# Half of the value products ahead of the transposes, and the scaled features made by ScalarE

## What is computed

```python
h = (node_features @ W_proj.T).reshape(B, N, H, dh)
scores = s_left[:, :, None, :] + s_right[:, None, :, :] + adjacency[..., None] * we
scores = leaky_relu(scores, 0.2) + (NEG * (adjacency <= 1e-05))[..., None]
agg = einsum('bijh,bjhd->bihd', softmax(scores, axis=2), h).reshape(B, N, D)
out = leaky_relu(node_features + agg + bias, 0.5)      # then x + out, and a layer norm
```

## Time and profile before

| | |
|---|---|
| median of 3 runs | 1983.24 us (1981.75 to 1984.76) |
| the profiled execution | 1981.11 us |
| its span | 1979.2 us |
| POOL busy | 1866.3 us (94%), 663 instructions |
| DVE busy | 1821.9 us (92%) |
| PE busy | 1795.4 us (91%) |
| ACT busy | 1646.4 us (83%), 3895 instructions |

### The profile page before, as it was taken

How to read it: one execution, slowest core, us unless ns; L and a number is a source line. 1 busy time by engine, 2 the same in 40 slices (tenths; PEclk the granted TensorE clock), 3 DMA queues, 4 the chain that set the end, 5 groups by cost and what they waited for, 6 DMA issues and landing times.

```text
span 1979.2 us, 34310 instructions
## 1 busy us (share of the span) xinstructions
PE 1795.4 (91%) x11080; PEld 875.2 (44%) x11080; DVE 1821.9 (92%) x3413; ACT 1646.4 (83%) x3895; POOL 1866.3 (94%) x663
## 2 busy tenths in 40 slices
PE   7799999999999999899999999999999999878885
PEld 6544444444444444445444444444444444333332
DVE  3699999999999999999999999999999999999997
ACT  6788887899888898888988889888887898676674
POOL 3599999999999999999999999999999999999995
PEclk9899999999999999999999999999999999999999
DMA  3232315233243243333233331333315233333310
GB/s 100 73 115 91 102 50 157 83 114 106 66 138 99 81 120 100 94 113 99 79 120 100 86 119 58 121 121 91 102 54 156 81 113 91 102 96 96 102 54 11
DMA packets 138090, 190.63 MB, mean 96 GB/s; under 512 B 22328, under 2 KB 56504, under 8 KB 137912
## 3 DMA queue, kind: packets, MB, share of 16 engines
q1 hardware_dynamic: 137912, 188.44, 31.8%
HBM read 179.77 MB, written 8.65 MB: 95 GB/s over the span
## 4 chain that ended last, share of the span: by engine, by line
POOL 28%; ACT 20%; PE 19%; issue 17%; DVE 15%; SPq 0%; DMA 0%; ACTq 0%; DVEq 0%; POOLq 0%
POOL X L501 26%; PE psum L1217 15%; DVE X L1102 11%; ACT E L773 4%; PE psum L1396 3%; ACT psum L776 3%; ACT pen L734 3%; ACT squares L642 2%; DVE X L1091 2%; POOL haug L484 1%; ACT blk L590 1%; ACT blk L563 1%; ACT x1s L670 1%; ACT o_sb L670 0%; ACT act_T L563 0%
## 5 line engine op out<-in xcount | busy, mean ns | idle before, releaser
L501 POOL TENSOR_TENSOR X<-RHO,E 128x1536 f32<-128x1536 f32 (+1 forms) x512 | 1779.3, 3506 | 41.8 <-ACT E L773 35.3
L1102 DVE SCALAR_TENSOR_TENSOR X<-psum,s_j,X 128x512 f32<-128x512 f32 x2048 | 1397.4, 741 | 78.8 <-POOL X L501 68.0
L1217 PE MATMUL psum<-X,haug 128*33 128x512 f32 x4096 | 978.6, 598 | 8.2 <-ACT accU L752 4.6
L1396 PEld LDWEIGHTS psum<-ident,adj_sb 128*128 128x128 f32 x2048 | 285.9, 140 | 561.8 <-DVE X L1102 429.1
L1396 PE MATMUL psum<-ident,adj_sb 128*128 128x128 f32 x2048 | 430.6, 291 | 101.3 <-DVE X L1102 97.7
L773 ACT ACTIVATE E<-psum,we_s 128x512 f32<-128x512 f32 x512 | 395.5, 772 | 139.0 <-PE psum L1217 137.1
L1217 PEld LDWEIGHTS psum<-X,haug 128*33 128x33 f32 x4096 | 195.0, 110 | 431.7 <-issue 390.6
L776 ACT ACTIVATE psum<-psum,we_s 128x512 f32<-128x512 f32 x512 | 380.7, 744 | 0.0
L1217 PE MATMUL psum<-sgn_ident,pen 128*128 128x128 bf16 x2048 | 374.7, 219 | 0.0
L734 ACT ACTIVATE pen<-adj_sb,pen_bias 128x512 bf16<-128x512 f32 x512 | 366.8, 717 | 1.0 <-PE psum L1217 0.2
L1091 DVE TENSOR_TENSOR X<-psum,E 128x512 f32<-128x512 f32 x496 | 334.0, 673 | 3.6 <-ACT RHO L563 2.2
(11 more groups left out here) (231 smaller groups left out, 1547.5 us busy)
## 6 DMA issues: line engine op xcount, KB each, us to landing
adj_sb<-in_adj_dram SPq DMA_DIRECT2D x128, 1024.0 KB, 5.2
RHO<-rho_scratch SPq DMA_DIRECT2D x31, 1024.0 KB, 9.7
out_dram<-o_sb SPq DMA_DIRECT2D x32, 256.0 KB, 2.3
xg<-in_x_dram SPq DMA_DIRECT2D x28, 256.0 KB, 5.3
blk<-in_adj_dram SPq DMA_DIRECT2D x56, 64.0 KB, 5.1
X<-in_x_dram SPq DMA_DIRECT2D x2, 256.0 KB, 3.0
W_sb<-in_L_gnn_W_dram SPq DMA_DIRECT2D x4, 64.0 KB, 2.1
X<-in_adj_dram SPq DMA_DIRECT2D x4, 64.0 KB, 2.8
```

Source lines behind the costliest of these rows:

```text
L501: Q.tensor_tensor(X[m % NX][:, 0:heads, :], RHO[:, g % 2, 0:heads, :], bc(E[m % NE][:], 1, [P, heads, GROUP]), ALU.mult).then_inc(B_pool, 1)
L1102: ins = V.scalar_tensor_tensor(slot[:, h, :], TA[m % NT], s[:, k, h:h + 1], slot[:, h, :], ALU.mult, ALU.max)
L1217: return T.matmul(o, l, r, start=start, stop=stop)
L1396: T.matmul(o, adj_sb[c][:, t, at:at + P], ident[:], is_transpose=True, start=True, stop=False)
```

## The change

Four things:

- `values` is cut in two. `values(m, 0)`, heads 0 and 1, stands in front of TensorE's wait for `X_sb` and so in front of the transposes; it waits for a new semaphore, `X_half`, that DVE sets after head 1. The wait for `accU_sb` goes with it. `values(m, 1)`, heads 2 and 3, stays behind the host's pieces and sets `pv_done`.
- `make_haug` moves from POOL to ACT: one copy with a per-partition scale for each column tile and head, 128 x 32, so 64 instructions a batch. They are spread over the slots n = 59 to 65 and 70 to 76, four a slot, eight in n = 62 and 73. For the first batch 16 come before the first slot and 16 in each of the slots 1, 2 and 3. The semaphore counts column tiles now, and a wait for it on ACT is added ahead of each copy of h.
- the two slots in which POOL does all four heads move from 11 and 29 to 22 and 36.
- the tables are drawn up anew, mostly by one slot.

```diff
-    FOUR = (11, 29)
+    FOUR = (22, 36)
-    AT_PE = {"xT": (-26, -20, 0, 18), "wh0": (-26, -17, 0, 18), "wh1": (-24, -16, 5, 19), "ST": (-11, 7, 20, 29),
+    AT_PE = {"xT": (-27, -22, 0, 18), "wh0": (-26, -18, 0, 18), "wh1": (-25, -16, 5, 19), "ST": (-11, 6, 20, 29),
...
-    AT_ACT = {"xT": (-24, -16, 2, 20), "wh0": (-23, -15, 6, 21), "wh1": (-21, -13, 9, 22),
+    AT_ACT = {"xT": (-24, -17, 2, 20), "wh0": (-23, -15, 5, 21), "wh1": (-22, -13, 8, 22),
-          "z_rstd": (0, 19, 28, 39), "r_rstd": (3, 22, 37, 44), "r_norm": (6, 24, 40, 49), "x1T": (7, 29, 46, 50),
-          "h0": (10, 29, 46, 52), "h1": (13, 31, 48, 52)}
+          "z_rstd": (0, 17, 29, 40), "r_rstd": (4, 20, 36, 45), "r_norm": (7, 24, 40, 49), "x1T": (8, 29, 46, 51),
+          "h0": (10, 29, 46, 52), "h1": (11, 32, 49, 52), "haug": (59, 62, 70, 73)}
-    AT_POOL = {"xb": (-24, -8, 20, 25), "r_shift": (5, 24, 39, 45), "haug": (58, 59, 62, 65)}
+    AT_POOL = {"xb": (-20, -7, 19, 23), "r_shift": (6, 21, 38, 45)}
...
-    EPI_PE = {"back0": 2, "back1": 3}
+    EPI_PE = {"back0": 1, "back1": 3}
-    EPI_POOL = {"shift": 15}
+    EPI_POOL = {"shift": 13}
...
+            def make_haug(nb, k):
+                if k == 0:
+                    act.wait_ge(v_sb, nb + 1)
+                    if nb >= 2:
+                        act.wait_ge(pv_done, BODY * (nb - 1))
+                for h in range(H):
+                    ins = copy(haug[nb % 2][:, k, h, 0:DH], hb[:, k, h * DH:(h + 1) * DH], v_j[:, k, h:h + 1])
+                ins.then_inc(haug_sb, 1)
...
+            for k in range(CHUNK):
+                make_haug(0, k)
             for m in range(-BODY // 2, 0):
                 host(m)
...
+                if 0 < m < CHUNK:
+                    for k in range(CHUNK * m, CHUNK * (m + 1)):
+                        make_haug(0, k)
                 penalty(m + LEAD)
...
+                    if h == 1:
+                        ins.then_inc(X_half, 1)
...
+                values(m, 0)
                 pe.wait_ge(X_sb, m + 1)
                 if m + NT < MT:
                     transposes(m + NT)
...
-                values(m)
+                values(m, 1)
```

More of the change, by code:

```diff
@@ L58, in build_program @@
-    AT_DVE = {"max": (-20, -13, 12, 26), "rin": (-18, -6, 16, 27), "res": (1, 19, 30, 42)}
-    AT_POOL = {"xb": (-24, -8, 20, 25), "r_shift": (5, 24, 39, 45), "haug": (58, 59, 62, 65)}
[2 rows of a table added]
+    AT_ACT = {"xT": (-24, -17, 2, 20), "wh0": (-23, -15, 5, 21), "wh1": (-22, -13, 8, 22),
+          "logits": (-21, -13, 9, 24), "exp": (-19, -11, 13, 27), "soft": (-14, -5, 19, 30), "ST": (-9, 11, 23, 33),
+          "oT": (-7, 13, 24, 35), "y1": (-6, 14, 25, 36), "y2": (-5, 14, 26, 36), "ssq": (-4, 17, 28, 39),
+          "z_rstd": (0, 17, 29, 40), "r_rstd": (4, 20, 36, 45), "r_norm": (7, 24, 40, 49), "x1T": (8, 29, 46, 51),
+          "h0": (10, 29, 46, 52), "h1": (11, 32, 49, 52), "haug": (59, 62, 70, 73)}
@@ L60, in build_program @@
+    AT_DVE = {"max": (-20, -13, 11, 26), "rin": (-16, -7, 14, 29), "res": (1, 19, 30, 43)}
+    AT_POOL = {"xb": (-20, -7, 19, 23), "r_shift": (6, 21, 38, 45)}
     ONCE_PE = {"rmT": 52, "Rb": 53, "rhoT": 55, "hsum": 56}
-    ONCE_ACT = {"diag": 55, "factors": 57, "rho": 58, "hcol": 61}
-    ONCE_DVE = {"rm": 52, "R4": 54, "lam": 55}
+    ONCE_ACT = {"diag": 55, "factors": 56, "rho": 58, "hcol": 62}
+    ONCE_DVE = {"rm": 53, "R4": 54, "lam": 55}
     ONCE_SP = {"rho": 49}
-    EPI_PE = {"back0": 2, "back1": 3}
+    EPI_PE = {"back0": 1, "back1": 3}
@@ L65, in build_program @@
     EPI_ACT = {"acc": 2, "prelu": 7, "rstd": 10, "norm": 15}
-    EPI_DVE = {"part0": 4, "part1": 5, "lky": 6}
-    EPI_POOL = {"shift": 15}
+    EPI_DVE = {"part0": 3, "part1": 5, "lky": 6}
+    EPI_POOL = {"shift": 13}
     EPI_SP = {"store": 15, "rho": 8}
@@ L309, in build_program @@
         B_dve = sem("B_dve")
+        X_half = sem("X_half")
         X_sb = sem("X_sb")
@@ L476, in first_residual @@
                 Q.tensor_tensor(x1_of(c)[:], x1_of(c)[:], xb[set_of(c)], ALU.add).then_inc(r_first, 1)
[L478 to L485, removed]
             def epi_shift(g):
@@ L514, in host @@
                             r_shift(c)
-                        if n == AT_POOL["haug"][u]:
-                            make_haug(nb, u)
             Q.memset(wlr[:], 0.0).then_inc(const_set, 1)
@@ L543, in _ @@
                 first_residual(c)
-            for q in range(NC_):
-                make_haug(0, q)
             for m in range(-BODY // 2, 0):
@@ L689, in chain_h @@
                 act.wait_ge(h_ps[j], c + 1)
+                if c >= NB and j == 0:
+                    act.wait_ge(haug_sb, JT * (c // NB - 1) + CHUNK * (c % NB + 1))
                 if c % NB == 0 and j == 0 and c > 0:
-                    act.wait_ge(haug_sb, NC_ * (c // NB))
                     act.wait_ge(sig_sb, c // NB)
@@ L829, in host @@
                             chain_h(c, 1)
+                        if 0 <= n - AT_ACT["haug"][u] < CHUNK:
+                            make_haug(nb, CHUNK * u + n - AT_ACT["haug"][u])
                     if n == ONCE_ACT["diag"]:
@@ L1398, in transposes, with values @@
                 ins.then_inc(adjT_ps, 1)
-            def values(m):
+            def values(m, r):
                 g, k = divmod(m, JT)
[L1402 to L1409, removed]
+                if r == 0:
+                    pe.wait_ge(X_half, m + 1)
+                    if g % NB == 0:
+                        pe.wait_ge(haug_sb, JT * (g // NB) + k + 1)
+                    if k == 0 and g % NB == 0:
+                        pe.wait_ge(hden_sb, g // NB + 1)
+                    if k == 0 and g > 0:
+                        pe.wait_ge(accU_sb, g)
+                    if m == 0:
+                        pe.wait_ge(acc_zero, 1)
+                for h in (2 * r, 2 * r + 1):
                     rows = slice(64 * (h % 2), 64 * (h % 2) + HA)
-                    ins = mm(ACC[h // 2][rows, :], haug[(g // NB) % 2][:, k, h, :], X[m % NX][:, h, :],
+                    ins = mm(ACC[r][rows, :], haug[(g // NB) % 2][:, k, h, :], X[m % NX][:, h, :],
                              start=(k == 0), stop=(k == JT - 1))
-                ins.then_inc(pv_done, 1)
+                if r == 1:
+                    ins.then_inc(pv_done, 1)
             def epi_back(g, r):
```

2 lines of the change are left out of this document (removed), and 4 rows, old and new, of the table AT_PE.

## The result

The changed kernel takes **2061.74 us** (median of 3 runs, 2060.89 to 2067.11) against 1983.24 before: a ratio of **1.040, 95% interval 1.038 to 1.043**. It is slower by 78 us. I had said 1992, with a range up to 2008: the sign was right, the size far off. The profiled execution has a span of 2059.1 us.

A forecast was written before the change was run, and what follows sets the result against it. It took POOL, with small hold-ups by ACT, as the bound. 11.5 + 11 - 8 - 4 - 1 = +9.5 us on 1981.1 gave 1990.6, stated as 1992 us; own range 1984 to 2003, chance 0.45, a tenth over 2008.

The forecast's parts named there:

- Part 3: Value products in front: nothing in common slots, 2.4 us of ACT idleness at slot 0 of six bodies, -0.9 us at the end.
- PE is late as well at every start of a group: Rival: PE late at all group starts, 31 times 0.5 to 1 us, giving 2015 us; chance 0.10.
- The second stretch and the tables (-8): The 45 slots outside the transition: half of POOL's idle time goes, -1.2 us in each of 7 bodies, -8 us.
- Start (+11.5): Program start: haug copies on ACT delay E and POOL's fourth X; +11.5 us, bounds 8.7 to 15.
- The price of a copy (0.21): Each small haug copy on ACT takes 0.21 us, bounds 0.17 and 0.27; 13.4 us a batch.
- The rival that they don't: Rival: ACT's small copies don't overlap, 0.31 us each, 43 us on top, giving 2035 us; chance 0.04.
- The transition (+1.8 each): The 19 slots from 58: ACT becomes the bound, 72.8 us against 71.0, +1.8 in each of six, +11 us.
- The cover that I "had already spent": POOL's shift two slots earlier removes only waits of ACT; counted at nothing, as ACT's stretch already ran with no other waits.
- The last transition (-4.3): Into the last body, with no chain on ACT: copies hidden, POOL's 4.3 us come off, entered as -4 us.
- The end (-0.9): Very end of the program: pv_done comes 0.95 us sooner, -0.9 us.

The follow-up runs named there:

- no_order: The changed kernel with the first half of the value products behind the transposes again; haug on ACT and the new tables stay: 2004.11 us.
- order_alone: The kernel before with the new order of the value products alone; haug on POOL and the tables as before: 2022.78 us.
- tables_alone: The kernel before with the new tables alone; haug on POOL at its old slots, value products whole and behind: 1978.40 us, ratio 0.9978.
- last_on_act: The kernel before with new tables, only the last batch's haug on ACT, heads 0 and 1 in front in the very last slot only: 1975.01 us, ratio 0.9964.
- no_order_first_pool: no_order with the first batch's haug made on POOL ahead of the loop; ACT keeps the other seven batches: 1990.76 us.
- order_acc1: order_alone with ACT's copy of accU one slot earlier, ahead of E: 2036.73 us.

## Why the prediction was wrong, step by step

**The step that failed** is in Part 3: "At k = 0 it isn't zero", right, but "queued there, in the slot 0 of six bodies". I worked the wait out only where ACT had been made late, and took the other 25 group starts for common slots, at nothing. The wait doesn't need a late ACT. `accU` can't be copied before the last values of the group are there, and the copy takes 1.27 us; the earlier trace rows shows that ACT stood ready for it at 24 starts (the 25th wait is the end). With nothing between the two ends on PE, PE must idle at least that long at each start. Measured: 31 waits of 2.4 us (the shortest 1.46), and the order costs 57.6 us where I had 14.4 - 0.9 = 13.5. By place, the 25 starts that I had at nothing cost 43.6 us, nearly all of it at the 21 with a start at slot 16, 32 or 48 of the first seven bodies. The six that I had worked out cost 14.9, as forecast, and that is in part luck: ACT waited 3.4 us in slot 2 (20.4 in 6) where I had said 1.6, and of the 14.9 us an estimated 7 to 8 are the lower clock (27 us at it against 10 in no_order, at 0.43 to 0.47), which my sum hadn't in it.

The rival "PE is late as well at every start of a group" had the place right, at 0.5 to 1 us a start, and 0.10 of the chance. The price is 1.3 us a start on average with haug on POOL and 1.9 in the changed kernel, but it isn't even: nothing at the starts of the last body, 3.6 at slot 48 with the tables of before. What I held against it, that POOL waited 1.0 us for PE, looks at the wrong pair: PE's lateness reaches POOL through ACT's E (in the changed kernel E waited 148.0 us for PE, and POOL's X 141.6 us for E). ACT's wait in the earlier trace rows would have told that PE would come to wait, but not the price: in the kernel before it stands at the starts of the last body and at slot 0, where order_alone loses nothing, and is missing at slot 48, where PE already waited 0.8 us for ACT and where the order costs most.

**The second stretch and the tables (-8).** POOL's idle time was to fall by half. The tables alone bring 3.5 us over the whole kernel, and the first stretch of no_order is at 167.0, as before: with haug on ACT there is nothing of the -1.2 a body. In the changed kernel's body 3 it is +7.4, all of it the order.

**Start (+11.5): right.** POOL's timeline in the changed kernel, beside the earlier trace rows:

```profile
97.79 3.44 POOL L493 TENSOR_TENSOR X<-RHO,E 128x1536 f32<-128x1536 f32 x1 [13.41 <-ACT E L772]
103.22 3.45 POOL L493 TENSOR_TENSOR X<-RHO,E 128x1536 f32<-128x1536 f32 x1 [1.98 <-ACT E L772]
```

13.41 us where I had said 13.5, then 1.98 against 0.90. In tables_alone these are 3.87 and 0.46 us, together 11.1 less; putting the first batch back on POOL gave 13.4.

**The price of a copy (0.21): right.**

ACT's timeline at the first of them, and the group of all 512:

```profile
81.99 3.52 ACT L551 ACTIVATE haug<-hb,v_j 128x32 f32<-128x32 f32 x16
```
```profile
L551 ACT ACTIVATE haug<-hb,v_j 128x32 f32<-128x32 f32 x512 | 120.9, 331 | 0.0
```

Sixteen end after 3.52 us, with 0.33 for the last one: (3.52 - 0.33) / 15 = 0.213 us from start to start. A single copy lasts 0.331 us, so in a row they overlap. The rival that they don't is out.

**The transition (+1.8 each): the bound right, the size not.** ACT was to become the bound of the 19 slots. In no_order it is busy 69.42 of 71.9 us, 97%, with POOL at 65.78. In tables_alone, with haug on POOL, it is the other way:

```profile
1003.40:1072.80 69.40, 62.88 (x394) 29.81 (x394) 65.18 (x118) 56.81 (x130) 68.52 (x27) 1.00 0.46 137
```

I had 72.4 us of work for ACT less 2.0 of lead, 70.4 and a gain of 0.6 without the order. ACT's work was less (69.4), but it also waited 2.5 us where I had let it wait for nothing: no_order's bodies of about 239 us are 2.2 longer than the 236.7 of tables_alone, +13 in six where I had -3.6. The cover that I "had already spent" wasn't there. With the order the transition is 74.6.

**The last transition (-4.3): half of it. The end (-0.9): right.** From slot 45 of body 6 to slot 13 of the last body, no_order and last_on_act both take 112.8 us, 2.2 less than tables_alone; the 4.3 us of work left POOL there, and half came off the time. Behind POOL's last X, last_on_act is 1.1 us shorter.

**The sum for no_order.** Without the order's terms my forecast would be 1992 - 13.5 = 1978.5; it measures 2004.1. The 26 us between are the tables (4.5), six transitions (17), the last one (2) and the start (2, if no_order_first_pool's 13.4 is taken for it).

**What stays open.** The clock's share. Between 110 us and the last slot PE had 63 us at the lower level in the changed kernel, 14 in no_order and none before. At 0.43 to 0.47 us each that is 21 to 23 of the 57.6 us of the order, and 27 to 30 of the whole 78. It is an estimate from the price of three groups; no run held the clock and kept the ring. At the start and the end the changed kernel has another 47 us at the lower level against 32 before, whose price no run shows. Why haug on ACT with the old tables costs 55.6 us and not 25.7 wasn't followed by a run: the traces show 34 us of it in the six groups that start a body, where the clock is low for 37 us, and 14.5 before slot 13 of the first body. What makes PE able to take up a wait at some starts and not at others wasn't tested. Nor was any version tried in which a third accumulator bank takes the new group's values, which might break the ring.

## What to carry to other kernels

An in-order engine that waits for a copy of what it has just produced is in a ring: the first instruction of a loop's next round that needs the copy must have enough independent work ahead of it to cover the copy and the other engine's current instruction (at slot 16 of body 3, 1.25 us of copy and 0.63 of an E). Before moving such an instruction forward, list every round in which its semaphore is waited for, not only those where something is late, and look at both ends there in the trace: the partner waiting for the engine (24 starts) or the engine already waiting for the partner (slot 48 of six bodies). Either pointed to a round at which PE then stood (all 31 in order_alone, 1.46 to 3.9 us). Whether it costs time has to be asked of each place: here the same wait of 1.46 us cost 1.1 to 1.3 us at slots 16 and 32 of order_alone and nothing in the last body.

## What the runs showed of the hardware

In the changed kernel the granted clock fell to 0.50 of full speed behind an idle time of PE of only 2.02 us between busy stretches, and was low for 3.4 of the 4.9 us from 896.5 to 901.4; the same idle time at slot 16 of three other bodies left it at full. One such dip, beside a wait of 2.0 us, made a group 1.6 us longer than the same group with the same wait at full clock (63.0 against 61.4 us). In the changed kernel the mean granted clock is 0.974, and 0.992 before. A kernel with waits on PE of 1.46 us each in their place (order_acc1) kept 0.992.

Small copies on ACT overlapped: one of 128 x 32 lasts 0.33 us, and sixteen in a row followed each other 0.213 us apart.
